# A mixture-of-experts block on one core: where TensorE turns the former expert's output rows, ahead of the branch to an expert's body or inside it

## The reference, cut to what matters

```
x = x + 0.5 * ffn(layernorm(x))
x = x + mixer(layernorm(x))          # 5 projections, a running sum over tokens, a 3-tap convolution
x = x + 0.5 * ffn(layernorm(x))

ffn: logits = tokens @ gate.T ; top1 = argmax(logits)           # 8 experts
     each expert takes its first 320 tokens (C = 1.25 * 2048 / 8)
     hmid = gelu(tokens_of_e @ wi[e])       # 512 -> 2048
     eout = hmid @ wo[e]                    # 2048 -> 512
     out[token] = softmax weight of the chosen expert * its row of eout
```

## Time and profile before

| | |
|---|---|
| median of three runs | 1097.07 us |
| the profiled execution | 1096.42 us, of which 1094.7 us is the span from the first to the last instruction |
| TensorE matmul busy | 1044.4 us, 95% |
| VectorE, ScalarE, GpSimd busy | 721.1, 543.7, 144.3 us |
| mean granted TensorE clock | 0.977 of full speed |
| share of the chain that ended last | TensorE 90%, VectorE 4% |

### The profile page before, as it was taken

One profiled execution on the slowest core, in us unless ns is written; L12 is line 12 of the kernel. 1 busy time (PEld: TensorE's weight loads), 2 busy tenths in 40 slices (PEclk: granted clock), 3 DMA queues, 4 the chain that ended last, 5 costly groups with the idle time before them and its releaser, 6 DMA issues.

```text
span 1094.7 us, 20908 instructions
## 1 busy us (share of the span) xinstructions
PE 1044.4 (95%) x7888; PEld 987.2 (90%) x7888; DVE 721.1 (66%) x1091; ACT 543.7 (50%) x851; POOL 144.3 (13%) x138
## 2 busy tenths in 40 slices
PE   9699999999999999599999996999999999999995
PEld 6699999999999999378777776999999999999995
DVE  8556565776577686477786774557777777665552
ACT  5445455565556565253342324355665656554441
POOL 3201111203021110100000022002212021130101
PEclk9899999999999999899999996999999999999998
DMA  8468546566464761500011244437566575664510
GB/s 309 176 240 303 185 173 215 181 222 206 161 235 156 251 208 38 178 1 1 1 39 39 80 144 147 153 116 244 202 229 213 190 244 185 228 211 142 169 39 25
DMA packets 83276, 177.32 MB, mean 162 GB/s; under 512 B 4192, under 2 KB 4704, under 8 KB 83168
## 3 DMA queue, kind: packets, MB, share of 16 engines
q1 hardware_dynamic: 75488, 152.61, 40.6%
q0 software_dynamic: 7168, 23.07, 6.0%
q10 hardware_dynamic: 576, 1.05, 0.3%
HBM read 162.04 MB, written 18.87 MB: 165 GB/s over the span
## 4 chain that ended last, share of the span: by engine, by line
PE 90%; DVE 4%; DMA 2%; issue 1%; ACT 1%; POOL 1%; POOLq 0%; ACTq 0%; SPq 0%; DVEq 0%
PE psH L1226 13%; PE psH L1227 13%; PE psH L1228 13%; PE acc L1234 12%; PE acc L1235 12%; PE acc L1233 12%; PE acc L1226 3%; PE acc L1228 3%; PE acc L1227 3%; DVE row_stats L831 1%; PE psH L1357 1%; PE psH L1458 1%; DVE dtl L798 1%; PE psT L1286 1%; PE psT L1559 1%
## 5 line engine op out<-in xcount | busy, mean ns | idle before, releaser
L1226 PE MATMUL psH<-dth,wih 128*128 128x240 f32 (+5 forms) x1024 | 295.0, 288 | 0.0
L1234 PE MATMUL acc<-htl,woh 128*128 128x240 f32 (+5 forms) x1024 | 293.4, 287 | 0.0
L1227 PE MATMUL psH<-dtl,wih 128*128 128x240 f32 (+5 forms) x1024 | 293.4, 287 | 0.0
L1235 PE MATMUL acc<-hth,wol 128*128 128x240 f32 (+5 forms) x1024 | 293.2, 286 | 0.0
L1228 PE MATMUL psH<-dth,wil 128*128 128x240 f32 (+5 forms) x1024 | 293.2, 286 | 0.0
L1233 PE MATMUL acc<-hth,woh 128*128 128x240 f32 (+5 forms) x1024 | 293.2, 286 | 0.0
L798 DVE TENSOR_TENSOR wol<-raw_wo,woh 128x1024 fp32r<-128x1024 f32 x128 | 155.7, 1223 | 146.6 <-ACT woh L615 143.5
L649 ACT ACTIVATE gel<-psH 128x320 f32<-128x320 f32 x256 | 111.8, 437 | 189.1 <-PE psH L1228 178.8
L615 ACT ACTIVATE woh<-raw_wo 128x1024 fp32r<-128x1024 f32 x128 | 134.6, 1059 | 132.3 <-PE acc L1235 132.1
L1226 PEld LDWEIGHTS psH<-dth,wih 128*128 128x128 f32 x1024 | 193.1, 189 | 0.4
L1227 PEld LDWEIGHTS psH<-dtl,wih 128*128 128x128 f32 x1024 | 193.0, 188 | 0.0
(11 more groups left out here) (195 smaller groups left out, 1145.4 us busy)
## 6 DMA issues: line engine op xcount, KB each, us to landing
raw_wi<-in_wi SPq DMA_DIRECT2D x64, 1024.0 KB
raw_wo<-in_wo SPq DMA_DIRECT2D x64, 1024.0 KB, 5.4
out_x<-xt SPq DMA_DIRECT2D x4, 1024.0 KB, 5.9
xt<-in_x SPq DMA_DIRECT2D x6, 512.0 KB, 8.2
xt<-x SPq DMA_DIRECT2D x3, 1024.0 KB, 9.7
raw_u<-in_wuT SPq DMA_DIRECT2D x1, 1024.0 KB
raw_u<-in_wvT SPq DMA_DIRECT2D x1, 1024.0 KB
xt<-in_x ACTq DMA_DIRECT2D x2, 256.0 KB, 3.8
```

What stands on the lines that cost most here:

```text
L1226: pe.matmul(out, lh, rh, start=first, stop=False)
L1227: pe.matmul(out, lh, rl, start=False, stop=False)
L1234: pe.matmul(out, lh, rl, start=False, stop=False, skip_group_check=True)
L1235: return pe.matmul(out, ll, rh, start=False, stop=False, skip_group_check=True)
```

## The change

`turn_out(e)` leaves the loop head, where it stood between `turn_tokens` and `dispatch`, and becomes the first thing in an expert's body, behind the branches and ahead of the wait for `dt_lo`. Its instructions and its waits are the same. It stood in the code twice for each layer (the narrow and the wide head), and now stands six times, once in each body.

```
@@ -1470,6 +1470,7 @@
                 def expert(e, w, s=s):
+                    turn_out(e)
                     pe.wait_ge(s.dt_lo, DC * e + 3)
                     clear_acc()
                     turn_rest()
@@ -1506,7 +1507,6 @@
                                 if c < 2:
                                     pe.wait_ge(s.eoT_done, DC * e + c + 1)
                                 turn_tokens(e, c, chunks)
-                            turn_out(e)
                             dispatch(what, ks)
```

## The result

| | before | after |
|---|---|---|
| median, both on the same chips | 1096.91 us (6 runs, 1093.5 to 1099.37) | 1149.26 us (6 runs, 1147.7 to 1153.65) |
| ratio, with its 95% interval | | 1.0479 (1.0455 to 1.0502) |
| profiled execution, span | 1096.42, 1094.7 us | 1149.93, 1148.2 us |
| mean granted TensorE clock | 0.977 | 0.961 |

The forecast was 1097.5 us and the range 1093.5 to 1101.5. The time came out 47.8 us above the range.

A forecast was written before the change was run, and what follows sets the result against it. TensorE was taken as the bound (90% of the chain), with gaps possible only at 16 expert beginnings. 14 x 0 + 0 + 0.4 us on 1096.42 gave 1096.8; the runs' median lies 0.65 higher, so 1097.5 us, range 1093.5 to 1101.5.

The forecast's parts named there:

- The order by itself: Warm expert beginnings: moving the branches ahead of the eight transposes costs nothing, as the sequencer runs ahead of the array.
- 14 x 0 us: The 14 later expert beginnings: dispatch stays hidden beside running TensorE work, 0 us each.
- The bound of +4.2 us: Upper bound at warm beginnings if branches emptied the array's queue: 2.9 us at five wide, 1.3 us at nine narrow.
- +0.4 us: First layer's first expert: a hole in turn_out's transposes while the next code is fetched, taken between 0 and 1.0 us.
- if the code came no earlier than now: First layer's first expert: next code arriving only at 45.3, as before the change, giving a hole of 2.65 us.
- code that is not there when it is wanted: Rival: 14 warm beginnings need a fetch of 2.3 to 3.5 us, 0.4 to 1.6 us each; 1103 to 1119 us; chance 0.06.
- The rival of a clock kept down: A 2.65 us hole at the first expert delays the clock's rise, about 1.3 us more; 1100 to 1102 us; chance 0.10.
- The rival by which dispatch is on the path: Dispatch delays every beginning now, so moving it saves 0.57 us x 14 = 8 us; 1089.5 us; chance 0.04.

The follow-up runs named there:

- Pad 21: Kernel before, turn_out still in the head, unused places put in front of each visited body so the visit's entry stands at 247; 1131.92 us, ratio 1.0335.

## Why the prediction was wrong

**The step that failed** is this one: "The kernel's layout wants at most 255, so that the last place of a block is left for the visit. That still holds, closely. The visited bodies stay where they are." My count was near enough (about 225 and 245; they are 227 and 247 by the text, 223 and 243 by the records), and the limit was wrong. I took from `addr_align` that only the branch at place 255 has to find room, and left the visit's entry out: a branch lands on it, and it stands directly behind the body. The runs put the highest harmless place for it at 242 (239 by the records). From 243 on the kernel fetches 18 to 23 pieces more. Read with the threshold, the simplest account is that the entry is then put into the next block, so that a visited body takes two blocks, and the second layer's experts take 13 blocks (the loop's and six times two) in place of 7; the visit no longer lands in the block that holds the body, and the blocks don't all stay. The packets and the threshold are shown; where the entry is put, and that blocks push each other out, is concluded from them. A mere count of blocks is not enough: the changed kernel stalls at the 16th expert on the body that had just run at the 15th, and the kernel with shorter bodies stalls on one of them with its entry at a harmless place.

**The order by itself** costs nothing, as predicted. 14 x 0 us: at the nine warm beginnings without a stall `mm1` comes 2.95 to 2.99 us behind the last `mm2`, before 2.93 to 2.97, some 0.3 us over all nine. The bound of +4.2 us, for branches that empty the array's queue, did not come about. What I missed is that the order can matter once a fetch is needed. `turn_out` in the head is 1 us of work that runs beside the fetch. In the body it stands behind the fetch. Pad 21 has the same entry as the changed kernel (one place more by the records) and costs 37 us; the change costs 52.4. In the profiled executions the first `mm1` of the first layer stands 6.3 us later in pad 21 and 11.0 us in the changed kernel, that of the second 31.8 and 45.2 us. Not all of this need be the order: the unvisited bodies are longer in the changed kernel too, and no run takes the two apart.

**The first expert.** +0.4 us was the sum, out of 0 to 2.65. The place was right (a hole inside the eight transposes, behind the first four rather than the first three) and the size near the upper bound: 2.31 us with the entry out of the way, 1.46 us with three pieces in the body. The row that answers is the upper bound's, "if the code came no earlier than now". The term that was mis-sized is the fetch: 2.3 to 3.5 us, counted from the entry to the body. The 2.3 us of the earlier trace rows run only from where the sequencer got stuck. Counted from the body's first record the next piece took 4.7 us there (40.6 to 45.3), and 5.2 us with the entry out of the way (40.6 to 45.8). In the changed kernel itself this place costs 11.0 us, the two holes of 3.12 and 2.68 us and 4.55 us ahead of the tokens:

```profile
44.62 1.54 PE L1407 MATMUL acc<-ident,dn 128*128 128x128 f32 x6 [13.46 <-issue]
50.56 0.66 PE L1451 MATMUL psT<-ident,eoT 128*128 128x128 f32 x4 [3.12 <-issue]
53.89 1.01 PE L1451 MATMUL psT<-ident,eoT 128*128 128x128 f32 x4 [2.68 <-issue]
```

In the earlier trace rows the same transposes at L1407 waited 8.78 us, for ScalarE's `dn`. The 13.46 us are in the main the two visits of the first layer, which end 2.4 us later than before, and the 3.3 us for which the sequencer stands still at the head of the loop. The gathering of the tokens, done at 40.06, hides the visits alone, as before, but not both.

**The rivals.** The second one, "code that is not there when it is wanted", named the mechanism, with a chance of 0.06 and 1103 to 1119 us. Its chance was too low for a step that rested on a count against a limit which no row showed; the Trainium skill's rule (named there) spoke for it, and the trace now agrees, with branches of 4.2 to 4.8 us at the five warm beginnings that stall. Its price was wrong in three ways. It had 14 warm beginnings at 0.4 to 1.6 us; five stalled, with 2.9 to 3.9 us of idle time and 3.3 to 5.2 us each in all, 22.8 us. It had nothing for the visits and the first experts of the layers, which are 11.9 + 11.9 us and nearly all of the 7.1 ahead of the second layer. And it had no clock, which is in all of these: 10.1 us of longer matmuls.

The rival of a clock kept down did not come true at its own place: with the entry out of the way the hole at the first expert was 2.31 us, and the kernel lay 2.1 us behind at `mm1` and 2.0 us at that expert's last `mm2`, so nothing was paid in clock on top. That this kernel's whole 4.2 us of span lie in the rival's range is chance; more than half of it is the added jump. Clock was lost behind the stalls of the changed kernel, which the rival did not have. The rival by which dispatch is on the path has nothing for it.

**Open.** Why the last 16 places (by the records) are closed to the entry, though not to the body's instructions. Which pieces are held at a time: no run separates the length of the unvisited bodies from the order, or shows what a fetch pushes out.

## What to carry to other kernels

Where code is laid out by blocks, count every place that a branch lands on, also the one directly behind a body, and leave room behind it: here 13 places of 256 were too few with the entry at 243, 14 were enough (16 and 17 by the records' count). Read the packets of the instruction queue first; they said 27 or 50 where the busy times said nothing. Keep work that can run without the branch's target in front of the branch, since it covers a late target, and treat a step that "just fits" as a chance of its own, priced at all places that share the layout.

## What the runs showed of the hardware

- A branch of the dispatch takes 0.07 to 0.21 us at a beginning without a stall (the three records above at 106.7). At the five warm beginnings with one, the longest takes 4.2 to 4.8 us (the fifth expert's record above, 4.2 us at the sixth, and these of the branch behind the chain of tests), and a visit takes up to 7.7 us:

```profile
L1492 PEldq COMPARE_BRANCH  x4: 351/4515/4764, 414.7 to 1071.4; - x4
```

- More than four blocks of TensorE's code stay held in the kernel before: between 104 and 444 us the instruction queue brings nothing, while the bodies of five widths run (304, 272, 240, 288 and 256 columns, some 223 instructions each). The Trainium skill (Runtime: NRT & Kernel Launch, section "Instruction fetch mechanics") gives TensorE 2048 instructions, which is eight blocks, and says beside it that the memory is only two cache lines. The trace is in keeping with the former and not with the latter. That all seven blocks of the second layer's experts stay held is not shown, and the stall of the kernel with shorter bodies at its 15th expert speaks against it.
- A hole of 3.60 us in front of the fifth expert was followed by a granted clock of 0.74 over 5.2 us. In pad 21 one of 2.59 us at the same expert was followed by 1.00 (its window, columns as above). So a stall that is a microsecond shorter can save more than the microsecond; the two kernels also differ in order:

```profile
263.20:268.40 5.20, 5.20 (x42) 5.20 (x41) 4.52 (x7) 2.18 (x4) 3.25 (x2) 1.00 0.08 13
```
